# Two fused transformer layers on one core: the start-up reordered (first roots, row and weight centring, second half's root, code loads) and every place number set anew

## The reference, cut to what matters

```
xn = layernorm(x)
x  = x + attn0(xn) + ffn0(xn)
xn = layernorm(x)
x  = x + attn1(xn) + ffn1(xn)

attn0: h = xn @ Win.T + bin                      # width 64, 4 blocks:
       h = h + sconv(silu(ln(h))) * scl          # complex decay, written as rotate, scan, rotate back
       h = h + W2 @ silu(W1 @ ln(h) + b1) + b2
       out = ln(h) @ Wout.T + bout
ffn0:  silu(xn @ gate.T * gs) * (xn @ up.T * us) @ down.T * ds      # codes -1, 0, 1; width 1792
attn1: xn @ (weight masked by blocks).T + bias
ffn1:  ((silu(xn@U1@V1g + b) * (xn@U1@V1u + b)) @ U2) @ V2 + b2     # rank 128, width 1376
```

## Time and profile before

| | |
|---|---|
| time, median of 3 runs | 305.98 us (305.81 to 306.9) |
| the profiled execution, own time | 305.49 us |
| its span | 303.6 us |
| PE busy | 291.7 us, 96% |
| DVE, POOL, ACT busy | 175.8, 159.2, 118.4 us |
| granted clock of PE over the span | 0.977 |

### The profile page before, as it was taken

How to read it: one execution, slowest core, us unless ns; L and a number is a source line. 1 busy time by engine, 2 the same in 40 slices (tenths; PEclk the granted TensorE clock), 3 DMA queues, 4 the chain that set the end, 5 groups by cost and what they waited for, 6 DMA issues and landing times.

```text
span 303.6 us, 4378 instructions
## 1 busy us (share of the span) xinstructions
PE 291.7 (96%) x1573; PEld 194.3 (64%) x1573; DVE 175.8 (58%) x270; ACT 118.4 (39%) x197; POOL 159.2 (52%) x184
## 2 busy tenths in 40 slices
PE   6888989999999999999999999989999999999995
PEld 4785547665565657556565655646577888788784
DVE  3784796565725784684545745678887622333303
ACT  1552345453634132444635535223045730146500
POOL 4878259995391311155474284630467585047650
PEclk9795899999999999999999999999999999999999
DMA  7999618108000212010110011210020000200003
GB/s 256 328 286 208 101 35 124 33 1 121 2 0 2 69 36 71 0 35 13 37 35 26 2 35 38 69 35 2 0 69 1 3 1 32 73 35 0 0 2 138
DMA packets 11749, 17.86 MB, mean 59 GB/s; under 512 B 848, under 2 KB 6224, under 8 KB 11728
## 3 DMA queue, kind: packets, MB, share of 16 engines
q1 hardware_dynamic: 6624, 12.49, 12.7%
q0 software_dynamic: 4960, 4.98, 10.1%
q10 hardware_dynamic: 144, 0.12, 0.1%
HBM read 20.46 MB, written 2.10 MB: 74 GB/s over the span
## 4 chain that ended last, share of the span: by engine, by line
PE 85%; POOL 6%; DVE 4%; issue 2%; DMA 1%; ACT 1%; DVEq 0%; POOLq 0%
PE bank L593 15%; PE bank L594 15%; PE bank L690 15%; PE bank L561 8%; PE bank L563 8%; PE bank L562 8%; PE bank L652 5%; PE bank L624 3%; PE bank L630 2%; PE bank L555 2%; DMA early<-in_params 1%; PE bank L643 1%; PE bank L642 1%; PE bank L615 1%; POOL root L1079 1%
## 5 line engine op out<-in xcount | busy, mean ns | idle before, releaser
L1162 POOL TENSOR_TENSOR hidl<-hid,hidh 128x512 f16<-128x512 f32 x28 | 33.3, 1189 | 47.8 <-ACT hidh L756 47.6
L593 PE MATMUL bank<-xh,gatew 128*128 128x512 f16 (+1 forms) x136 | 45.5, 353 | 2.6 <-ACT XT L785 1.4
L594 PE MATMUL bank<-xl,gatew 128*128 128x512 f16 (+1 forms) x136 | 45.4, 353 | 0.0
L593 PE MATMUL bank<-xh,upw 128*128 128x512 f16 (+1 forms) x136 | 44.8, 348 | 0.0
L594 PE MATMUL bank<-xl,upw 128*128 128x512 f16 (+1 forms) x136 | 44.8, 348 | 0.0
L690 PE MATMUL bank<-downw,hidh 128*128 128x512 f16 x112 | 42.5, 380 | 0.0
L690 PE MATMUL bank<-downw,hidl 128*128 128x512 f16 x112 | 42.4, 379 | 0.0
L1168 POOL TENSOR_TENSOR actl<-hid,acth 128x512 fp32r<-128x512 f32 (+1 forms) x22 | 28.7, 1307 | 25.9 <-ACT acth L763 25.7
L1079 POOL TENSOR_TENSOR root<-var,powers 128x4 f32<-128x4 f32 (+1 forms) x25 | 23.6, 949 | 23.5 <-DVE var L942 19.9
L830 ACT ACTIVATE silu<-bank,early 128x512 f32<-128x512 f32 x28 | 19.2, 687 | 41.1 <-PE bank L594 41.1
L1011 DVE SCALAR_TENSOR_TENSOR hid<-bank,early,silu 128x512 f32<-128x512 f32 x28 | 21.0, 751 | 19.8 <-PE bank L594 19.3
(11 more groups left out here) (158 smaller groups left out, 607.1 us busy)
## 6 DMA issues: line engine op xcount, KB each, us to landing
X<-in_x SPq DMA_DIRECT2D x8, 256.0 KB, 5.6
out_x<-X SPq DMA_DIRECT2D x8, 256.0 KB, 2.0
downw<-in_down POOLq DMA_DIRECT2D x2, 896.0 KB, 8.3
stage<-in_v SPq DMA_DIRECT2D x6, 256.0 KB, 2.6
stage<-in_mask SPq DMA_DIRECT2D x4, 256.0 KB, 7.0
upw<-in_up POOLq DMA_DIRECT2D x1, 1024.0 KB, 11.9
gatew<-in_gate POOLq DMA_DIRECT2D x1, 1024.0 KB, 12.5
stage<-in_weight SPq DMA_DIRECT2D x4, 256.0 KB, 2.6
```

The costliest lines, as they stand in the source:

```text
L593: pe.matmul(bank_of(key)[:, c], w, xh[b][:, k, c], start=(k == 0), stop=False)
L594: mm = pe.matmul(bank_of(key)[:, c], w, xl[b][:, k, c], start=False, stop=(k == KT - 1))
L1162: pool.tensor_tensor(hidl[:, n % FT, :], hid[:, n % UNITS, :], hidh[:, n % FT, :], ALU.subtract).then_inc(hid_lo, 1)
```

## The change

It has five parts. In the prologue the first two roots go ahead of the seed, and load 0 goes between them and the seed. `rows` and `centre win` leave the dense part and go between the low parts of tiles 1, 2 and 3 in the prologue. In the dense part all of grow, seed 3 and turn stand behind step 0, and there the four statistics and the root of half 1 follow them, ahead of load 3 (up, place 0.5) and load 2 (gate, place 4.6); load 3 stood between the growths before, and load 2 too. On SP the loads of the staging buffers from the fifth on and the load of bc wait until load 0 has landed. And every other place number is new: the jobs are the same, many stand a step or more earlier or later.

```
-    place(W2_AT, [[("rows",), ("centre", "win")], [("centre", "w2")]])
+    place(W2_AT, [[("centre", "w2")]])
...
-PROLOGUE = ((("seed", 0), ("stats", 0), ("stats", 1), ("norm", 0), ("seed", 1), ("norm", 1), ("stats", 2)),
-            (("xt", 0), ("codes", 0), ("load", 0), ("norm", 2), ("seed", 2), ("stats", 3), ("grow", 0)),
+PROLOGUE = ((("stats", 0), ("stats", 1), ("load", 0), ("norm", 0), ("seed", 0), ("stats", 2), ("norm", 1), ("seed", 1)),
+            (("xt", 0), ("codes", 0), ("norm", 2), ("seed", 2), ("stats", 3), ("grow", 0)),
             (("xt", 1), ("codes", 1), ("first", 0, 0), ("norm", 3), ("load", 1), ("grow", 1)),
-            (("xt", 2), ("first", 0, 1), ("xcopy", 0), ("first", 1, 0), ("grow", 2), ("grow", 3)),
-            (("xt", 3), ("first", 1, 1), ("xcopy", 1), ("first", 2, 0), ("first", 2, 1), ("xcopy", 2),
+            (("xt", 2), ("rows", 0), ("first", 0, 1), ("xcopy", 0), ("first", 1, 0), ("grow", 2), ("grow", 3)),
+            (("xt", 3), ("centre", 0), ("first", 1, 1), ("xcopy", 1), ("first", 2, 0), ("first", 2, 1), ("xcopy", 2),
...
-LOAD_AT = (0.2, 0, 7.1, 16.2)
-GROW_AT = (0, 0, 0.1, 0.5, 0.5, 0.5)
-LN_AT = (0.1, 1.1, 1.2, 1.4, 1.7, 4.1, 4.4, 5.0, 6.4)
-TABLE_AT = (5.3, 7.8, 8.1, 13.3)
-XT_AT = (4.5, 6.6, 8.9, 9.3)
-XCOPY_AT = (7.5, 8.0, 9.1, 9.9)
+LOAD_AT = (4.6, 0.5, 6.8, 20.6)
+GROW_AT = (0, 0, 0, 0, 0, 0)
+LN_AT = (0, 0, 0, 0, 0, 3.0, 3.9, 5.2, 5.9)
+TABLE_AT = (5.6, 6.7, 7.2, 10.7)
+XT_AT = (4.3, 6.0, 8.9, 9.0)
+XCOPY_AT = (6.4, 6.4, 9.6, 10.6)
...
             for t in range(TPB, 2 * TPB):
                 sp.dma_start(X[:, t, :], x[t]).then_inc(x_in[t], 16)
+
+            sp.wait_ge(codes_in[0], 16)
             for n in range(FIRST_LOADS, NSTAGE):
                 load(n)
```

More of the change, by code:

```diff
@@ L163, in build_order @@
                       "codes": [("cast", "gate", t), ("cast", "up", t)], "seed": [("seed", t)],
-                      "first": [("first", t, *f)], "load": [("load", t)], "grow": [("grow", t)]}.get(kind, [(kind, 0, t)])
+                      "first": [("first", t, *f)], "rows": [("rows",)], "centre": [("centre", "win")], "load": [("load", t)], "grow": [("grow", t)]}.get(kind, [(kind, 0, t)])
     order.append(("decay",))
@@ L186 @@
 U1_AT = 85
-LOAD_AT = (0.2, 0, 7.1, 16.2)
-GROW_AT = (0, 0, 0.1, 0.5, 0.5, 0.5)
-LN_AT = (0.1, 1.1, 1.2, 1.4, 1.7, 4.1, 4.4, 5.0, 6.4)
-TABLE_AT = (5.3, 7.8, 8.1, 13.3)
-XT_AT = (4.5, 6.6, 8.9, 9.3)
-XCOPY_AT = (7.5, 8.0, 9.1, 9.9)
-W1_AT = (6.6, 8.8)
-W2_AT = (0.2, 8.9)
-WOUT_AT = (33.0,)
-XBIAS_AT = (12.8, 24.7)
-MASK_AT = (33.2, 38.1, 40.4, 41.8, 42.9)
-U1_CAST_AT = (45.4,)
-V1_AT = (47.0, 51.8, 56.6, 60.3, 65.9, 68.2)
-U2_AT = (71.5, 73.1, 75.0)
-CHAIN_AT = ((2.0, 5.6, 7.3, 8.8, 10.0, 11.4, 13.1, 13.6, 15.3, 18.3, 20.5, 21.4, 21.9, 25.6, 27.7, 30.7, 30.9, 32.2, 33.7, 36.6, 37.6, 38.5, 42.3, 43.2, 45.2, 46.3, 47.8, 50.7, 51.5, 55.0, 55.0, 58.4, 59.3, 61.7, 62.3, 64.4, 66.1, 70.9, 71.0, 72.8, 74.4, 75.1), (12.5, 14.2, 15.5, 15.8, 18.6, 20.9, 23.3, 24.4, 25.1, 28.4, 28.6, 31.6, 33.0, 35.5, 37.6, 38.1, 38.6, 41.0, 42.7, 43.7, 45.3, 46.8, 50.7, 52.4, 53.2, 54.5, 56.8, 58.7, 60.8, 63.1, 64.2, 66.2, 68.6, 69.5, 71.4, 74.1, 75.0, 77.7, 78.3, 78.6, 82.3, 82.9))
@@ L202 @@
-WMASK_AT = (66.5, 72.9, 75.6, 77.1)
-W_AT = (82.6, 83.5, 85.8, 87.1)
-LN1_AT = ((75.9, 76.2, 76.7, 77.8, 77.8, 77.8, 78.4, 78.4, 78.6, 80.1, 80.9, 82.1, 82.6), (82.4, 86.5, 87.3, 90.1, 90.9, 91.8, 92.2, 93.6, 94.1, 95.4, 96.5, 97.2, 98.6))
-YBIAS_AT = ((102.3, 102.5, 104.7, 105.4), (110.8, 115.5, 122.1, 127.2))
-V2_AT = (88.3,)
+LOAD_AT = (4.6, 0.5, 6.8, 20.6)
[3 more added lines that the diff above has]
+XT_AT = (4.3, 6.0, 8.9, 9.0)
@@ new lines @@
+XCOPY_AT = (6.4, 6.4, 9.6, 10.6)
+W1_AT = (6.6, 7.7)
+W2_AT = (8.9,)
+WOUT_AT = (31.8,)
+XBIAS_AT = (22.6, 29.8)
+MASK_AT = (34.0, 37.2, 39.2, 40.6, 42.9)
+U1_CAST_AT = (45.6,)
+V1_AT = (47.2, 52.0, 56.7, 59.8, 65.0, 68.2)
+U2_AT = (72.9, 74.8, 75.2)
+CHAIN_AT = ((1.9, 5.6, 7.0, 7.8, 10.6, 11.7, 12.9, 14.2, 15.2, 17.2, 19.6, 21.9, 22.2, 26.7, 27.0, 28.4, 28.7, 33.7, 34.2, 35.6, 37.1, 38.3, 40.6, 44.3, 45.4, 45.6, 47.6, 50.4, 51.8, 53.1, 56.0, 58.0, 59.4, 61.9, 62.7, 63.6, 66.2, 69.4, 72.7, 73.4, 74.9, 75.4), (12.2, 14.8, 15.7, 15.7, 18.8, 20.0, 23.2, 23.9, 26.2, 27.9, 28.2, 31.4, 32.5, 35.1, 36.4, 38.4, 38.9, 40.7, 42.7, 44.6, 46.3, 46.4, 50.7, 52.8, 53.2, 53.6, 56.0, 58.7, 60.2, 63.0, 64.7, 66.8, 68.3, 70.3, 71.3, 74.8, 75.2, 77.1, 78.1, 78.7, 81.2, 82.9))
@@ L209, in place_psum @@
+WMASK_AT = (69.2, 71.1, 75.8, 77.0)
+W_AT = (82.4, 83.6, 85.2, 87.2)
+LN1_AT = ((75.8, 76.6, 77.1, 77.2, 77.6, 77.6, 77.6, 77.8, 77.8, 80.0, 80.7, 80.9, 82.4), (81.9, 86.7, 87.7, 90.7, 90.9, 91.4, 92.7, 93.3, 94.1, 95.2, 96.3, 97.8, 98.1))
+YBIAS_AT = ((99.0, 105.7, 107.2, 109.3), (117.1, 120.7, 125.8, 129.0))
+V2_AT = (88.8,)
 def place_psum(order):
```

## The result

| | before | after |
|---|---|---|
| time, median of 8 runs each | 305.88 us (305.76 to 306.9) | 308.05 us (306.82 to 309.45) |
| ratio, 95% interval | | 1.0075 [1.0051, 1.0098] |
| profiled execution, own time and span | 305.49, 303.6 us | 309.01, 307.1 us |
| PE busy, granted clock over the span | 291.7 us, 0.977 | 292.2 us, 0.972 |

The changed kernel is slower by 0.75%. The forecast was 303.0 us, 301.2 to 305.2. The profiled execution of after lies near the upper end of its eight, so its 3.5 us over the one of before is more than the medians show (2.2 us). All lines of after are numbered two higher than those of before.

The account below looks back on a forecast made before the run. POOL's list up to the root of half 1 was taken to bound the start, PE's own work all that follows. -2.64 - 0.34 = -2.98 us, from the profiled 305.49 to 302.5, so median 303.0 us; range 301.2 to 305.2.

Parts of the forecast that it names:

- term 2: Bank copies ahead of t1: PE's 1.36 us wait for XT goes, DVE is late next, so only 0.34 us won.
- Term 1: POOL's root of half 1 starts near 25.8 us, XN near 27.3, PE's transpose near 28.0: -2.64 us.
- the rule of the port: DVE and GpSimd exclude each other; XN would wait for load 3's issue, 0.5 us; left out of the sum.
- Half rate after the hole: PE's clock stays at half rate 2.6 us after the restart, as before; bounds -1.3 and +1.3 us.
- rival A: The longer PE hole keeps half rate to 33.3 us or beyond, plus a small new wait: 305.1 us; chance 0.2.
- the early `win`: `win` on PE needn't wait 1.2 us for late; cost at nothing, since PE waits for the root anyway.
- The remaining places: Jobs moved by a step or two, from 41 us on: no job loses cover, 0, bounds -0.8 and +1.5 us.
- SP's wait: Staging loads from the fifth on and bc wait for load 0: cover of 14 us, cost nothing.
- rival C: Gate's load of 8 tiles comes too late and PE waits 5.6 us: 308.6 us; 0.08 with other such waits.
- rival D: POOL isn't the bound; DVE's variance or PE's `win` is late, restart at 30 us or later: 305.5 us; chance 0.1.
- rows and centre between the low parts: In the prologue they take DVE time ahead of the last low part, where DVE had been waiting: cost nothing.
- Rival B: The clock never falls; PE restarts at full rate after the hole: -4.3, 301.7 us; chance 0.12.

Follow-up runs that it names:

- experiment 1: The changed kernel with all places behind the start set back to those before; new prologue, root, loads, growths and SP's wait stay: 305.31 us, ratio 0.9987.
- experiment 7: The kernel before with only the new prologue (first root ahead of the seed, load 0 earlier, rows and input weights between low parts): 307.59 us, 1.0081.
- experiment 11: experiment 1 with POOL held until two XN are written, either behind load 3's issue (303.68, repeated 303.78 us) or behind one low part, ahead of load 3 (304.15 us).
- experiment 2: The changed kernel with POOL held ahead of load 3 until the first two XN of half 1 are written: 306.42 us, ratio 1.0037.
- experiment 9: experiment 1 with POOL held ahead of load 3 until the first two XN of half 1 are written, run twice: 303.92 and 303.77 us.
- experiment 3: The changed kernel with rotation tables 1 to 3 at their places before: 309.61 us; also with POOL held until two XN are written (the hold): 308.4 us.
- experiment 12: The kernel before, first with POOL held behind its root of half 1 until two XN are written (305.55 us), then with unread matmuls in two holes (303.89 us).
- Experiment 6: The changed kernel with unread matmuls on PE, 18 ahead of the wait for XN and 12 ahead of the one for `z`: 305.01 us, 0.9989.
- experiment 4: experiment 1 with only the four table places as in the changed kernel: 307.29 us.
- experiment 10: experiment 9 with 13 unread matmuls in PE's hole ahead of half 1 (306.27 us); the second kernel also has ACT's two copies ahead of t1 (305.22 us).

## Why the prediction was wrong

The forecast was -2.98 us against before, and +2.2 was measured. By experiment 1 the miss has two parts of like size: the start, -2.64 forecast and -0.4 measured, and the places with term 2, -0.34 forecast and +2.7 measured.

**Term 1, the root: held; what follows from it did not.** The root came 2.36 us earlier, for 2.64. The late seed cost 1.0 us by the fourth root (13.01 for 12.02) and 1.3 by the root of half 1 in experiment 7, for 1.03; the moved issues and low part brought what I worked out. The step that failed is the next one: "XN near 27.3, PE's transpose near 28.0". I took XN at its undisturbed duration, and I left the rule of the port out of the sum on the strength of one row (XN at 9.92, 0.55 us beside an issue). That row was right for what it showed: an issue alone cost XN nothing there and 0.14 us in experiment 11. But behind load 3 stand a low part, a root and a low part with no gap, and beside those the pair takes 3.1 us more (4.25 for 1.13). In the order of before two roots stood there and only the second XN was caught (1.36 us); my trace of before showed it as a pair of 1.95 us, and I did not question it. The Trainium skill, in SBUF — State Buffer, "Who interferes with whom", says that DVE and GpSimd hold the shared ports against each other for a whole instruction. By that rule, the trace agrees: from 25 us on, each XN that was stretched by more than the issue's 0.14 us ends 0.3 us behind the end of one of POOL's low parts. And the rows show more: neither the end of the issue at 28.10 nor that of the root at 30.48 let the XN of the moment through, where POOL's next instruction began within 0.03 us. I weighed the rule for the wrong instruction. Price: 1.4 to 1.6 us by the medians of experiments 2 and 9; by the ratios only 1.2 and 0.4, since both kernels have executions at 307 and above.

**Half rate after the hole: the size was off.** I took 2.6 us and gave 5.3 as a bound; it was 5.4 us in the profiled execution. I had read one execution as if its length were the kernel's. This is PE's restart after the hole and its first matmul at full rate (0.38 us and not 0.63) in profiled executions:

| | hole | restart | first at full rate | between |
|---|---|---|---|---|
| before | 1.50 us | 30.65 | 33.51 | 2.9 us |
| after | 4.21 | 29.74 | 35.19 | 5.5 |
| experiment 1 | 4.46 | 29.74 | 34.41 | 4.7 |
| experiment 2 | 3.15 | 28.52 | 34.43 | 5.9 |
| experiment 3, without the hold | 4.64 | 29.81 | 33.07 | 3.3 |
| experiment 9, second time | 2.80 | 28.58 | 31.95 | 3.4 |

So with the new start the half rate lasted longer than before in each of them, but its length doesn't follow the hole's. That speaks against the reason that rival A (which I gave 0.2) gave for it, though its cost came about. What sets the length is not shown. Before itself is no fixed course either: in the profiled execution it is at 0.50 from 23.1 us on, ahead of the hole, while in the profiled execution of experiment 12's first kernel, the same up to there, the clock is 1.00 until 31.9 us. Experiment 6 shows that the two half-rate stretches of after together are worth 2.6 to 3.0 us. The hole was longer (4.2 us for 1.5) because of the slow pair and because PE came to it at 25.5 us instead of 29.1: `win` no longer waited, and the products behind it ran at full rate. I had noted the early `win` and cost it at nothing.

**Term 2, the bank copies.** The wait for XT went, and DVE was next, as said. But the low part of the last tile of half 1, which I wanted near 46 us, came at 51.13. And I gave "0 if DVE gets slower by its new neighbours" as the worst. It was not the worst: the scan took 2.05 us more, PE waited 2.7 us for `z`, and the clock fell again. The step that failed is DVE's list "with the same instructions" taken at its old durations.

**The remaining places: cost at 0, measured 2.7 us** (experiment 1 against after). Of this the places of the tables, 1 and 2 each a step earlier above all, are 2.0 us by the medians (experiment 4). The rest I put down to the second fall of the clock, which came only with the wait for XT gone as well (with that wait, `z` waits only 0.24 us); no run separates it. I asked which job loses its cover and looked at PE's waits; the cover that was lost was an idle stretch of POOL beside DVE's scan. My bound of +1.5 us ("two new waits of this size") was too small for that reason.

**What was right.** No wait for `late`; SP's wait and the late gate load cost nothing (gate landed in 10.3 us, PE waited for no codes: rival C did not happen); POOL was the bound (no idle time ahead of the root, against rival D); rows and centre between the low parts cost nothing that shows. Rival B, a clock that never falls, happened in no profiled execution without filled holes.

**The sum.** With POOL held beside XN and the old places the start is worth 1.7 to 2.1 us (experiment 11), not 2.64. What is still missing I put down to the hole of 3.4 us ahead of XN and the half rate behind it, since filling such holes gains in two kernels (6, 12); but filling it in the kernel of experiment 9 lost 2.4 us (10; 1.6 by the ratios), by a new collision, so that isn't shown.

## What to carry to other kernels

Before moving an instruction of POOL, look at what DVE does in the same microseconds, and the other way round: a job placed "earlier, under cover" can stretch the one that PE waits for to four times its time, and a start time on the chain says nothing without the neighbours of the instruction that follows. A wait of PE can cost twice, once for itself and once for the clock behind it, and how long the half rate lasts can't be read from one execution. Where the wait can't be removed try to fill it with matmuls that nobody reads: in the kernel before this gained nearly as much as the best version of the reordered start. An order tuned tightly around two engines that stretch each other must be measured after each step, because a gain in one place shifts the next collision.

## What the runs showed of the hardware

- Beside dense work of POOL, DVE's scan pair took 4.43 us for 1.39, a scaled product (L976) 2.49 for 0.75 (1.47 in before, beside a single low part), XN 2.27 for 0.55. Beside a single low part XN took 0.91, beside a root alone, in before, its ordinary 0.55. POOL is stretched too, less: a root 1.24 for 1.04 (after, 29.24), a low part 1.51 for 1.15 (before, 43.29).
- Executions of the same program differ: in experiment 2 the times lie in two groups, about 1 us apart at the nearest (only the first has a profile, without a second fall of the clock), and in experiment 10 (the first) the fall only moved to another place. With the holes filled in after, 12 executions lie within 0.41 us; with those of before filled, eleven lie within 1.93 us and one is 2.5 us above them.
- The Trainium skill, in TensorE: Matmul & The Clock Gate, "What's actually happening", has the throttled state as the default that activity releases. By this, the trace agrees: filled holes kept the granted clock at 1.00 (experiments 6 and 12), the unfilled ones of 4.2 and 2.8 us in after were each followed by 0.50. The length of a single hole doesn't decide it: `z`'s 1.83 us in experiment 2 and lno's 2.5 us in the second kernel of experiment 10 were not followed by a fall, the 1.68 us for `z` in the latter were.
